# Wide score steps for the running maximum, one search pass over both tiles, and a placing copy moved to ScalarE

## The reference

```python
x = x + attn(layernorm(x))          # 16 heads of width 8 share one k and one v; causal softmax
x = x + experts(layernorm(x))

# experts, per token and per head (8 heads):
q = rmsnorm(x) * gamma @ wq.T       # two halves of 64 per head
sim = q . keys                      # 32 scores per half: "x" list and "y" list
sx, sy = top_k(sim[0], 16), top_k(sim[1], 16)
scores = top_k(sx[:, None] + sy[None, :], 16)       # 16 best of the pair sums
h = gelu(xn . table_down[indices]) * softmax(scores)
out = sum(h * table_up[indices])
```

## Time and profile before

| | us |
|---|---|
| median of 3 runs | 955.2 (953.35 to 955.55) |
| the profiled execution | 956.12 |
| its span, from the first to the last instruction | 954.3 |

### The profile page before, as it was taken

The page is one execution under the profiler, slowest core; times in us unless marked ns, Lnnn a source line. Parts: engine busy times, 40 slices in busy tenths (PEclk is TensorE's granted clock), DMA queues, the critical chain, the costliest instruction groups (busy, mean ns, idle before and its releaser), DMA issues.

```text
span 954.3 us, 21078 instructions
## 1 busy us (share of the span) xinstructions
PE 729.4 (76%) x6014; PEld 466.6 (49%) x6014; DVE 788.2 (83%) x2998; ACT 712.5 (75%) x1041; POOL 635.9 (67%) x371
## 2 busy tenths in 40 slices
PE   4574669697878878796978788787879797877464
PEld 3332326364555646463645556464646464554333
DVE  3217199898989899899989899998989898988776
ACT  1334498797979797988979797979889797958381
POOL 2012059595978869595949688695959595868561
PEclk9777799999999999999989999999999999988676
DMA  5321303021212204030212121030302121000000
GB/s 155 52 26 27 47 11 60 8 59 17 54 23 35 41 15 62 7 64 6 60 17 54 23 40 37 17 60 9 65 3 60 17 49 25 22 8 18 0 1 11
DMA packets 58160, 32.53 MB, mean 34 GB/s; under 512 B 5904, under 2 KB 57744, under 8 KB 57936
## 3 DMA queue, kind: packets, MB, share of 16 engines
q1 hardware_dynamic: 58128, 32.14, 18.7%
HBM read 19.93 MB, written 5.24 MB: 26 GB/s over the span
## 4 chain that ended last, share of the span: by engine, by line
issue 34%; PE 20%; POOL 18%; DVE 15%; ACT 8%; SPq 1%; DMA 1%; POOLq 1%; DVEq 0%; ACTq 0%
POOL acc L497 16%; DVE prob L1001 6%; PE score L1168 3%; DVE late_scores L853 3%; PE score L1292 3%; ACT late_scores L592 3%; PE misc L1268 2%; PE score L1305 2%; POOL pieces L484 2%; DVE halves L847 2%; ACT prob L698 2%; PE score L1171 2%; DVE acc L1013 1%; PE misc L1218 1%; PE score L1198 1%
## 5 line engine op out<-in xcount | busy, mean ns | idle before, releaser
L497 POOL TENSOR_TENSOR acc<-acc,prob 128x1024 f32<-128x1024 f32 x186 | 441.5, 2374 | 16.6 <-POOL acc L497 0.5
L1001 DVE SCALAR_TENSOR_TENSOR prob<-score,cut,prob 128x1024 f32<-128x1024 f32 x256 | 317.4, 1279 | 20.3 <-ACT prob L698 19.1
L698 ACT ACTIVATE prob<-score,neg_lse,unit 128x1024 f32<-128x1024 f32 x256 | 302.4, 1206 | 24.4 <-PE score L1292 21.1
L1292 PE MATMUL score<-sel,pieces_t 128*128 128x512 f16 x512 | 162.6, 402 | 70.5 <-DVE prob L1001 65.7
L497 POOL TENSOR_TENSOR acc<-prob 128x1024 f32<-128x1024 f32 x31 | 73.3, 2364 | 169.9 <-DVE prob L1001 169.9
L609 ACT ACTIVATE probs<-score 128x512 f32<-128x512 f32 x192 | 111.3, 597 | 46.7 <-PE score L1200 39.8
L1292 PEld LDWEIGHTS score<-sel,pieces_t 128*128 128x128 f16 x512 | 38.0, 101 | 138.4 <-DVE prob L1001 123.0
L1198 PE MATMUL score<-q_stack,k_stack 128*128 128x512 bf16 x192 | 76.2, 397 | 23.6 <-DMA q_stack<-max_t 16.1
L1168 PE MATMUL score<-k_ahead,q_ahead 128*128 128x256 bf16 (+1 forms) x512 | 80.5, 265 | 17.2 <-DMA q_ahead<-q_scratch 7.9
L1257 PE MATMUL score<-xn_kept,wdt 128*128 128x128 f32 x480 | 85.0, 278 | 4.4 <-DVE prob L1001 4.0
L592 ACT ACTIVATE halves<-score 128x512 bf16<-128x512 f32 x64 | 35.6, 594 | 69.2 <-PE score L1171 69.2
(11 more groups left out here) (131 smaller groups left out, 1468.7 us busy)
## 6 DMA issues: line engine op xcount, KB each, us to landing
q_ahead<-q_scratch SPq DMA_DIRECT2D x96, 64.0 KB
q_stack<-q_scratch SPq DMA_DIRECT2D x96, 64.0 KB
q_scratch<-qk_piece SPq DMA_DIRECT2D x16, 192.0 KB, 2.4
xin<-x SPq DMA_DIRECT2D x16, 128.0 KB, 4.1
xres<-x SPq DMA_DIRECT2D x16, 128.0 KB, 4.6
x_kept<-x SPq DMA_DIRECT2D x16, 128.0 KB, 2.0
out<-fin SPq DMA_DIRECT2D x16, 128.0 KB, 5.5
xn_kept<-xn_t SPq DMA_DIRECT2D x15, 128.0 KB, 2.0
```

The lines of the kernel that those rows point to most:

```text
L497: eng.tensor_tensor(acc[:, j, :], so_far, prob[:, j * FH + h, :], ALU.add).then_inc(acc_added, 1)
L698: eng.activation(prob[:, g, :], score[g % BUFS][:, :], ACT.Exp, bias=neg_lse[:, j, h:h + 1], scale=unit[:, :]).then_inc(prob_made, 1)
L1001: eng.scalar_tensor_tensor(prob[:, g, :], score[g % BUFS][:, :], cut[:, j, h:h + 1], prob[:, g, :], ALU.is_ge, ALU.mult).then_inc(prob_mas ...
L1292: ins = eng.matmul(score[g % BUFS][:, cols], pieces_t[:, j, h, :], sel[:, cols], start=True, stop=True)
```

## The change

Five things change together.

1. The maxima are made in six steps w of 1024 columns over `score[1]` and `score[2]` (`score[1 + w % 2]`), with one ScalarE copy of 1024 columns each. Since `score[1]` is also used by the output stage, step 0 waits for both `activate`s of batch i-1, and `acc_transposes(i-1, 1)` waits for the fifth copy.
2. On DVE, `select_keys(b)` searches all 32 lists of both tiles first and replaces after that. The copy of the tops into PSUM leaves DVE: `place_tops` on ScalarE copies both tiles' tops at once (256 columns), between the seventh and the eighth `att_exp`.
3. On DVE, `select_pairs(i, 1)` moves from behind `sum_best(i, 0)` to a place in front of `make_y`. Its last subtraction is split off as `shift_best`; for tile 1 it runs behind `gate(i-1, 1)`.
4. On PE, steps 0 and 1 of the maxima go in front of acc_transposes 0, steps 2 and 3 in front of project_y, 4 and 5 in front of piece_transposes 1; acc_transposes 1 comes behind that.
5. `xn_transpose` and `xn_back` go in front of `xhat_transpose` and `xhat_back` and, on ScalarE, in front of the first `pair_probs`.

```diff
...
-            def max_scores_back(b, u):
-                eng.wait_ge(max_scores, at(max_scores, b, u + 1))
-                if u == 0 and later(b):
+            def max_scores_back(b, w):
+                eng.wait_ge(max_scores, at(max_scores, b, w + 1))
+                if w == 0 and later(b):
                     eng.wait_ge(max_step, at(max_step, b, 0))
-                if u < 4:
-                    dst = halves[0][:, 4 * u:4 * u + 4, 0, :]
-                    src = att[u % 2][:, :].rearrange("p (h k) -> p h k", h=4)
+                src = score[1 + w % 2]
+                if w < 2:
+                    dst = halves[0][:, 8 * w:8 * w + 8, 0, :]
+                    src = src[:, :].rearrange("p (h k) -> p h k", h=8)
                 else:
-                    dst = late_scores[:, 2 * (u - 4):2 * (u - 3), :].rearrange("p h k -> p (h k)")
-                    src = att[u % 2][:, :]
+                    dst = late_scores[:, 4 * (w - 2):4 * (w - 1), :].rearrange("p h k -> p (h k)")
+                    src = src[:, :]
                 eng.activation(dst, src, ACT.Copy).then_inc(max_kept, 1)
             def max_back(b):
...
                 if j == 1:
                     eng.preload_act_table_set("natural_log_exp_and_others")
+            def place_tops(b):
+                eng.wait_ge(key_step, at(key_step, b, SEARCHES))
+                eng.activation(misc[1][:, 0:TILES * P].rearrange("p (j h k) -> p j h k", j=TILES, h=FH),
+                               ranked[:, :, :, RANK_X:RANK_Y + RANKED], ACT.Copy).then_inc(top_placed, 1)
             def best_exp(b, j):
                 eng.wait_ge(shifted_made, at(shifted_made, b, j + 1))
                 if not later(b):
...
             def iteration(i, d, f, a, m, p):
                 if a:
-                    for u in range(MAX_STEPS):
+                    for u in range(7):
+                        att_exp(i + 1, u)
+                if f:
+                    place_tops(i)
+                if a:
+                    for u in range(7, ATT_STEPS):
                         att_exp(i + 1, u)
                 if d and f:
                     activate(i - 1, 0)
...
                     max_scores_back(i + 2, 1)
                 if f:
                     best_exp(i, 0)
+                if m:
+                    max_scores_back(i + 2, 2)
+                    max_scores_back(i + 2, 3)
                 if a:
                     x2_back(i + 1)
-                if m:
-                    for u in range(2, 5):
-                        max_scores_back(i + 2, u)
                 if f:
                     pieces_back(i, 0)
                 if m:
-                    for u in range(5, 9):
-                        max_scores_back(i + 2, u)
+                    max_scores_back(i + 2, 4)
                 if f:
                     log_sum(i, 0)
                 if m:
-                    for u in range(9, MAX_STEPS):
-                        max_scores_back(i + 2, u)
+                    max_scores_back(i + 2, 5)
                 if f:
                     pieces_back(i, 1)
-                if p:
-                    xhat_back(i + 3)
+                if a:
+                    xn_back(i + 1)
                 if f and not a:
                     activate(i, 0)
                     activate(i, 1)
                 if f:
                     pair_probs(i, 0, 0)
-                if a:
-                    xn_back(i + 1)
-                if f:
                     best_exp(i, 1)
+                if p:
+                    xhat_back(i + 3)
+                if f:
                     pair_probs(i, 0, 1)
                     log_sum(i, 1)
                     pair_probs(i, 0, 2)
...
-            def select_keys(b, j):
...
+            def select_keys(b):
+                for j in range(TILES):
+                    value = held(eng, at(sim_kept, b, j + 1))
+                    eng.wait_ge(setup_dve, 1)
+                    eng.wait_ge(sim_kept, value)
+                    for col, a in ((RANK_Y, 1), (RANK_X, 0)):
+                        for h in range(FH):
+                            keys_of = sim[:, j, (2 * h + a) * KEYS:(2 * h + a + 1) * KEYS]
+                            eng.max(ranked[:, j, h, col:col + RANKED], keys_of).then_inc(key_step, 1)
+                for j in range(TILES):
+                    value = held(eng, at(key_step, b, j * LISTS + FH))
+                    eng.wait_ge(setup_dve, 1)
+                    eng.wait_ge(key_step, value)
+                    for h in range(FH):
+                        ys_of = sim[:, j, (2 * h + 1) * KEYS:(2 * h + 2) * KEYS]
+                        eng.match_replace(left[:, j, h, :], ranked[:, j, h, RANK_Y:RANK_Y + RANKED], ys_of,
+                                          LOWEST).then_inc(key_step, 1)
             def sum_pairs(b, j):
-                eng.wait_ge(key_step, at(key_step, b, (j + 1) * KEY_STEPS))
-                tops = ranked[:, j, :, RANK_X:RANK_Y + RANKED]
-                tops_x = tops[:, :, 0:RANKED]
-                placed = misc[1][:, 0:FH * 2 * RANKED].rearrange("p (h k) -> p h k", k=2 * RANKED)
-                eng.tensor_copy(placed, tops).then_inc(top_placed, 1)
-                eng.wait_ge(top_placed, at(top_placed, b, j + 1))
-                tops = placed
+                eng.wait_ge(key_step, at(key_step, b, SEARCHES + FH * (j + 1)))
+                eng.wait_ge(top_placed, every(top_placed, b))
+                tops_x = ranked[:, j, :, RANK_X:RANK_X + RANKED]
+                tops = misc[1][:, j * P:(j + 1) * P].rearrange("p (h k) -> p h k", k=2 * RANKED)
                 first_x, tops_y = tops[:, :, 0:1], tops[:, :, RANKED:2 * RANKED]
                 xs = sim[:, j, :].rearrange("p (h a k) -> p h a k", a=2, k=KEYS)[:, :, 0, :]
                 eng.tensor_tensor(near[:, :, 0:KEYS], xs, tops_y[:, :, 0:1].broadcast_to([P, FH, KEYS]),
...
                     eng.wait_ge(pair_step, value)
                     for h in range(half * FH // 2, (half + 1) * FH // 2):
                         eng.max(best[:, j, h, 8:16], cand[:, h, :]).then_inc(pair_step, 1)
-                n += 2 * FH
-                eng.wait_ge(pair_step, at(pair_step, b, n))
+            def shift_best(b, j):
+                eng.wait_ge(pair_step, at(pair_step, b, (j + 1) * PAIR_STEPS))
                 first = best[:, j, :, 0:1]
                 if j == 0:
-                    first = misc[1][:, FH * 2 * RANKED:FH * (2 * RANKED + 1)].unsqueeze(2)
+                    first = misc[1][:, TILES * P:TILES * P + FH].unsqueeze(2)
                     eng.tensor_copy(first, best[:, j, :, 0:1]).then_inc(first_placed, 1)
                     eng.wait_ge(first_placed, every(first_placed, b))
                 eng.tensor_tensor(shifted[:, j, :, :], best[:, j, :, :], first.broadcast_to([P, FH, TOPK]),
...
             def iteration(i, d, f, a, m, p):
                 if f:
-                    select_keys(i, 0)
-                    select_keys(i, 1)
+                    select_keys(i)
                     sum_pairs(i, 0)
                     select_pairs(i, 0)
+                    shift_best(i, 0)
                     sum_pairs(i, 1)
+                    select_pairs(i, 1)
                 if a:
                     make_y(i + 1)
                 if d:
...
                     ln1(i + 3)
                 if f:
                     sum_best(i, 0)
-                    select_pairs(i, 1)
                 if d:
                     gate(i - 1, 1)
                 if f:
+                    shift_best(i, 1)
                     log_sum_exp(i, 0)
                 if m:
                     fold_max(i + 2, 0, 3)
...
      ...
-            def scores_for_max(b, u):
-                if u == 0:
+            def scores_for_max(b, w, d=False):
+                if w == 0:
+                    eng.wait_ge(ahead_in, every(ahead_in, b))
+                    if d:
+                        eng.wait_ge(act_made, every(act_made, b - 3))
+                elif w == 1:
                     if later(b):
                         eng.wait_ge(att_probs, at(att_probs, b, 0))
-                    eng.wait_ge(ahead_in, every(ahead_in, b))
-                elif u > 1:
-                    eng.wait_ge(max_kept, at(max_kept, b, u - 1))
...
+                else:
+                    eng.wait_ge(max_kept, at(max_kept, b, w - 1))
+                for u in (2 * w, 2 * w + 1):
+                    bank = score[1 + w % 2][:, (u % 2) * BANK:(u % 2 + 1) * BANK]
+                    nh, nk, h0, j = (4, P, 4 * u, 0) if u < 4 else (2, T, 2 * (u - 4), 1)
+                    for n in range(nh):
+                        eng.matmul(bank[:, n * nk:(n + 1) * nk], q_ahead[:, h0 + n, j * P:(j + 1) * P],
+                                   k_ahead[:, 0:nk], start=n == 0, stop=False)
+                    late = bank.rearrange("p (n k) -> p n k", k=nk)[:, :, nk - P:nk]
+                    ins = eng.matmul(late, ident_bf, mask_q[:, 0:nh, :], start=False, stop=True)
                 ins.then_inc(max_scores, 1)
```

(33 more changed lines are left out.)

69 lines of the change are left out of this document (24 added, 45 removed).

## The result

| | before | after |
|---|---|---|
| median of 4 runs, us | 954.5 (953.35 to 955.55) | 920.2 (916.23 to 921.23) |
| ratio | | 0.9633, 95% interval 0.9602 to 0.9664 |
| span of the profiled execution, us | 954.3 | 918.3 |

A forecast was written before the change was run, and what follows sets the result against it. No engine was full, DVE had 3.7 us spare; the path ran from first search through gate 1 to first mask. Loop 13 x (52.25 - 49.85) = 31.2 plus 1.8 saves 33 us: median 955.2 to 922, range 910 to 943.

The forecast's parts named there:

- DVE up to make_y: DVE from first search T: copies leave, tile 1's selection (3.78 us) comes in; make_y at T+16.0 instead of T+12.8.
- The small operations: norm_x2's last two operations (L883, L886) wait for POOL; 1.89 us per iteration go, leaving 0.17 and 0.16 us.
- From y to gate 1: norm_x2 at T+18.5, a wide ScalarE copy 1.02 us, gate 1 at T+21.5 with DVE idle 0.7.
- From gate 1 to the first mask: POOL's xn and xhat meet the first fold, 0.6 us lost; first mask at T+28.2, 2.0 us earlier than before.
- Its 925 for a loss of 1.2: Alternative total if the folds lose both xhat operations, 1.2 us, by the skill's rule; losing none gives 913.
- The clock: PE's clock fell after a 2.8 us wait for POOL's pieces; that hole closes, returning nearly all 0.45 us per iteration.
- 1.00 in all windows: Expected sign: PE's granted clock at 1.00 in all windows of the loop.
- the fourth rival: Slower: xn_transpose waits for xn, PE stands over 2.8 us, the clock falls and key_scores runs cold; 971, chance 0.07.
- The ends: Outside iterations 1 to 13: iteration 0 gains 1.5, the prologue 0.3, iterations 14 and 15 0 within 0.5.
- POOL stays in the way: Rival: norm_x2's small operations meet POOL again, or log_sum held by sum_best keeps ScalarE standing; 935, chance 0.22.
- The folds win free: Rival: no exclusion at xhat, 2.6 us per iteration and the clock's 0.45; 913, chance 0.12.
- The change does not do what it says: Rival: ScalarE, not PE's waiting, already sets the pace from the copies to the eighth exp; 955, chance 0.05.

The follow-up runs named there:

- theory B of their run: Run: norm_x2's first small operation through PSUM, in the kernel before; theory B (DVE's queue sets the period) expected 930. Measured 956.07, ratio 1.0005.
- xhat first: The changed kernel with ln1 in front of norm_x2 on DVE and make_xhat in front of make_xn on POOL; 910.59 us, ratio 0.9543.
- with the small operation through PSUM as well: The changed kernel with ln1 and make_xhat moved ahead, plus norm_x2's first small operation through PSUM; 909.75 us, ratio 0.9525.
- section 3 of the experiments: The changed kernel with two more 512-column adds on POOL behind its sim pieces: 942.05; with norm_x2's first small operation through PSUM too: 940.70.
- the narrow-step kernel: The changed kernel with twelve 512-column maxima steps over score[2]'s two banks, in the new places, instead of six wide ones; 941.85 us, ratio 0.986.

## Why the prediction was right, point by point

The loop's gain came by the way that the prediction walked, with two errors in it (the worth of the small operations, and the clock). That the sum is right to 3 us is partly luck: the ends were wrong by up to 4.4 us each, and cancel.

- **DVE up to make_y.** T+16.0 forecast, T+15.6 measured; place_tops took 0.40 us (0.38 taken) and stayed hidden in the loop. In iteration 0 its cover was missing, and I had not looked there: the exps in front of it wait for a transfer, and DVE's pair sums waited 16.9 us behind them.
- **The small operations.** L895 and L898 are 0.17 and 0.16 us in all 16 executions, the 1.89 us forecast. But the prediction opens with them as if they set the time, which the earlier trace rows and the idle 0.84 before gate 1 do not support: in the old order they were worth nothing, and so were the copies. The sum came out because it followed gate 1 in the new order and not the savings. From the small operations alone one forecasts 930, as theory B of their run did, where 956 was measured.
- **From y to gate 1.** norm_x2 at T+18.0 (18.5 forecast), wide copies 1.02 (1.02), gate 1 at T+21.46 (21.5) with 1.03 idle (0.7).
- **From gate 1 to the first mask.** POOL's xhat met DVE as forecast: log_sum_exp took 0.58 where it was 0.22, and the fold 1.52 where its free size is 1.22, 0.66 together against 0.6 taken. By the rule of the Trainium skill, SBUF — State Buffer, Who interferes with whom, the one issued first wins. The trace agrees, one meeting at a time: POOL's multiplication started 0.20 us into the first fold and ended 0.47 behind that fold's end, 1.48 for 0.61; the second fold started while it ran and ended 1.08 behind it, 1.52 for 1.22. So the choice was not 1.2 or nothing, as the prediction had it; the folds lost the rest of an operation that was already running. Its 925 for a loss of 1.2 is also a slip: 13 x 0.6 = 8 us more is 930. First mask at T+28.0 (28.2).
- **The clock.** "1.00 in all windows" was wrong. So was tying the old falls to the wait of 2.8 us alone: iterations 2 to 12 of before all have it (2.75 to 2.81), among them, and the clock falls in five of these eleven. The hole in front of the pieces closed, but the new one that the fourth rival described is there in every second iteration, behind waits of 0.89 and 1.55 us and not behind one of 2.8. Its price is small: periods of about 49.66 with it and 49.50 without, 0.08 in the mean against the 0.05 taken, and it may be so small because DVE is still at its folds while key_scores runs cold; that is argued, not shown. In iteration 0 its effect came in full, by another wait than its condition names: xn_transpose waits 2.56 us for ScalarE's piece copy, not for xn, and xhat is waited for 2.16; the clock is 0.55 from 125 to 130, and key_scores takes 3.48 us. That iteration lost 2.9 us where 1.5 of gain were forecast. With xhat first the fall there lasts 6.8 us and the iteration takes 67.9, with the small operation through PSUM as well 3.4 and 65.9, which speaks for the clock as a cause; it is not shown apart.

```profile
125.00:130.00 5.00, 2.84 (x10) 1.23 (x9) 4.93 (x9) 3.24 (x7) 2.60 (x3) 0.55 0.00 0
```

- **The ends.** The tail gained 3.8 where 0 was forecast. POOL starts iteration 14's pieces at T+15.7 instead of T+17.1, but then waits 1.90 us for DVE's `bounded`, so its first add behind them comes only 0.4 earlier in the iteration; from there to iteration 15's, 52.85 us against 53.74, 0.9; and 2.5 lie behind that one, 37.66 us to the end against 40.16. No run takes this last and largest part to pieces. The prologue gained 1.0 (0.3). The loop gained 2.62 per iteration (2.40). The errors at the ends, -4.4, +3.8 and +0.7, cancel; the loop's +2.9 is what is left.
- **The rivals.** "POOL stays in the way" did not happen: the pieces ended 0.4 us before L895. Doing more on POOL on purpose (section 3 of the experiments) showed that its lateness costs by another way than this rival's, TensorE's wait for xhat. "The folds win free" did not happen here; the kernel with xhat first has free folds, because nothing of POOL meets them, at 910.6, against 913. "The change does not do what it says" did not happen: the waits in front of `halves` left the loop and the time fell.

What stays open: why exactly every second iteration falls to 1.2 GHz; in the narrow-step kernel the share of the copies' length was not separated from that of the banks' lead; and the exchange of xn and xhat on TensorE and ScalarE, the fifth part of the change, was never run alone or undone.

## What to carry to other kernels

Before pricing a saving on an engine, ask what releases that engine last downstream: 1.89 us of plainly wasted time per iteration were worth nothing while another chain released gate 1. Once three steps on TensorE had been moved in front of a wait, that edit and the copies' together gave 7.7 us. The 0.56 us of copies were idle time in front of y in both orders, and on the path (0.55) only where DVE comes to y last. A wait at the head of an in-order queue is priced by what stands behind it, so the cheapest edit is to put work that is ready in front of it (21 us here without removing anything, and again 10 us for ln1 and xhat). Walk a new order also through the first iteration, where the waits that hide a moved step may stand in front of it.

## What the runs showed of the hardware

- A small DVE operation that meets POOL waits for POOL's running operation and not for all its work: L895 took 0.61 us in the kernel with xhat first, beside a subtraction of 0.61 us on POOL; L910 took 0.60 with more work on POOL, the rest of an add of 1.30; against 1.15 in before, beside the first of two pieces. In the first two its successor ran free, 0.16.
- Either side can lose, whichever starts later: POOL's 256-column multiplication, started 0.20 us into the first fold, ran 1.48 us instead of 0.61, and the second fold, started while it ran, 1.52 instead of 1.22; in iteration 0 even the 2-column `rstd`, started 0.29 us into a fold, took 1.50 instead of 0.71.
- One 1024-column copy from PSUM to bf16 takes 1.02 us, two 512-column ones 1.08: the width itself saves 0.06 us a step. Most of what the narrow-step kernel loses (22 us) is in waits.
